# Chebyshev propagations two and three with fp16 pairs in place of bf16 triples

## The reference, cut to what matters

```python
deg = segment_sum(ones, src)                       # out-degree
dis = where(deg > 0, rsqrt(max(deg, 1)), 0)
wn  = -(dis[src] * dis[dst])
prop = lambda h: segment_sum(wn[:, None] * h[src], dst)

T0 = h                                             # relu(layernorm(x))
T1 = prop(T0)                                      # first propagation
T2 = 2 * prop(T1) - T0                             # second
T3 = 2 * prop(T2) - T1                             # third
feats = [sum(T[k] @ w[k]) + b for w, b in ((w2, b2), (w3, b3), (w4, b4))]
# softmax over the three, concatenate, fuse, batch norm, relu, add x
```

## Time and profile before

| | |
|---|---|
| time, median of 3 runs | 1339.63 us (1333.62, 1339.63, 1341.48) |
| span of the profiled execution | 1334.5 us (first to last instruction; no time of its own is listed for it) |
| busy TensorE / VectorE / ScalarE / GpSimd | 1089.8 / 974.4 / 691.7 / 599.0 us |
| propagations k = 1, 2, 3 in the span | from about 1028 to 1242 us |
| line 1324 (the propagations' matmuls, k = 0 to 3) | 2500 matmuls, 19% of the chain of waits |

### The profile page before, as it was taken

How to read it: one execution, slowest core, us unless ns; L and a number is a source line. 1 busy time by engine, 2 the same in 40 slices (tenths; PEclk the granted TensorE clock), 3 DMA queues, 4 the chain that set the end, 5 groups by cost and what they waited for, 6 DMA issues and landing times.

```text
span 1334.5 us, 23321 instructions
## 1 busy us (share of the span) xinstructions
PE 1089.8 (82%) x8345; PEld 633.6 (47%) x8345; DVE 974.4 (73%) x1600; ACT 691.7 (52%) x903; POOL 599.0 (45%) x343
## 2 busy tenths in 40 slices
PE   3878787787796888888788888837996999999893
PEld 2555554454461222222222222214696987788783
DVE  8677888886575999999999999918556535422466
ACT  7555565555446998999898999800000000000221
POOL 8532533422005998999999989960000000000000
PEclk9888878879796999999999999968997999999996
DMA  0100000000144111111112222110011000000201
GB/s 10 30 33 5 7 7 5 8 17 1 40 129 114 36 44 45 47 48 44 45 35 60 53 51 49 45 44 1 1 37 39 25 14 1 22 14 4 66 28 36
DMA packets 98907, 44.80 MB, mean 34 GB/s; under 512 B 85196, under 2 KB 96716, under 8 KB 98672
## 3 DMA queue, kind: packets, MB, share of 16 engines
q1 hardware_dynamic: 97104, 41.58, 11.8%
q0 software_dynamic: 1696, 1.74, 0.5%
HBM read 30.73 MB, written 12.56 MB: 32 GB/s over the span
## 4 chain that ended last, share of the span: by engine, by line
PE 50%; DVE 25%; issue 11%; ACT 5%; POOL 5%; DMA 2%; another core or an unknown queue 2%; SPq 1%; DVEq 0%; ACTq 0%; POOLq 0%
PE PS L1324 19%; DVE Eb L1150 15%; PE PS L553 10%; PE PS L557 8%; POOL Eb L982 3%; DVE Eb L1144 3%; PE PS L1709 3%; PE PS L1332 2%; ACT Eb L1115 2%; PE PS L1074 2%; PE PS L1064 1%; PE PS L1315 1%; ACT Eb L1117 1%; ACT Eb L1119 1%
## 5 line engine op out<-in xcount | busy, mean ns | idle before, releaser
L982 POOL TENSOR_SCALAR Eb<-Eb 128x1024 f32<-128x1024 f32 (+4 forms) x175 | 431.1, 2485 | 74.1 <-ACT Eb L1119 72.8
L1150 DVE SCALAR_TENSOR_TENSOR Eb<-Eb,PS 128x1024 f32<-128x1024 f32 (+4 forms) x350 | 366.7, 1084 | 16.7 <-ACT Eb L1117 10.5
L1324 PE MATMUL PS<-hs,CT 128*128 128x192 f16 (+3 forms) x2500 | 263.3, 267 | 4.0 <-DVE B L1557 1.8
L1119 ACT ACTIVATE Eb<-PS,small 128x1024 f32<-128x1024 f32 (+2 forms) x263 | 251.5, 997 | 28.0 <-PE PS L1064 24.5
L593 ACT ACTIVATE CT<-PS 128x500 f32 x313 | 183.7, 587 | 142.9 <-PE PS L557 135.1
L553 PE MATMUL PS<-mov,oneS 128*128 128x100 f16 x1565 | 184.6, 231 | 76.1 <-issue 71.0
L1324 PEld LDWEIGHTS PS<-hs,CT 128*128 128x128 f16 (+1 forms) x2500 | 227.5, 99 | 37.7 <-DVE SG L1557 2.7
L553 PEld LDWEIGHTS PS<-mov,oneS 128*128 128x128 f16 x1565 | 146.6, 107 | 157.9 <-issue 113.8
L1064 PE MATMUL PS<-Qb,Kb 96*128 96x512 f16 (+3 forms) x700 | 182.8, 364 | 11.1 <-ACT Eb L1119 7.2
L1074 PE MATMUL PS<-Eb,V 128*25 128x512 f32 (+3 forms) x1400 | 169.9, 558 | 3.4 <-DVE Eb L1150 1.8
L435 DVE TENSOR_TENSOR oneS<-iotaX,KL 128x2560 f16<-128x2560 int16 x80 | 120.1, 1501 | 71.6 <-PE PS L557 69.0
(11 more groups left out here) (258 smaller groups left out, 1006.6 us busy)
## 6 DMA issues: line engine op xcount, KB each, us to landing
Kb<-kd SPq DMA_DIRECT2D x168, 96.0 KB, 2.4
qd<-QH SPq DMA_DIRECT2D x12, 192.0 KB, 2.7
kd<-QH SPq DMA_DIRECT2D x12, 192.0 KB, 3.1
hs<-t_d SPq DMA_DIRECT2D x12, 192.0 KB, 2.5
Qb<-qd SPq DMA_DIRECT2D x4, 384.0 KB, 3.9
CT<-x_d SPq DMA_DIRECT2D x1, 1200.0 KB, 7.6
x_d<-B SPq DMA_DIRECT2D x6, 192.0 KB, 1.9
t_d<-A SPq DMA_DIRECT2D x6, 192.0 KB, 1.8
```

The source lines that it names most:

```text
L982: g.tensor_scalar(e, e, ELO, None, ALU.max).then_inc(S("floored"), 1)
L1119: a.activation(e, ps, ACT.Exp, scale=K.unsc[0:r, :]).then_inc(S("score_read"), 1)
L1150: v.scalar_tensor_tensor(out=e, in0=e, scalar=EHI, in1=cn, op0=ALU.min, op1=ALU.mult).then_inc(S("weighed"), 1)
L1324: m = p.matmul(bank(t % FIRST)[0:r, 0:w], K.CT[:, a, 128 * t:128 * t + r], hs[:, a, :, :].rearrange("p k d -> p (k d)"), start=(a == 0), s ...
```

## The change

In k = 2 and 3 the features are now given as two fp16 parts, 192 columns, as in k = 0 and 1. The scale is not the constant 4096 but a power of two for each of the two propagations, from a bound on the size of the values:

- `degrees` also finds the largest `dis` and the largest `dis` times in-degree of each partition (`K.peak`), three operations.
- k = 1's `first_term` finds the smallest value of each group's input (`K.tops`), and one more reduction follows after the seventh group.
- `turn_peaks` on TensorE, after `prop_first`, turns `K.peak` into a row in bank 6 (two transposes for k = 1, one for k = 2).
- `peak_row` on VectorE, after tile 0 of k = 1 and of k = 2, reduces that row to one number and works out the scale and its inverse with single-element operations.
- `spread_scale` on TensorE, after tile 7 (t == 1 of the loop), copies both to all partitions with a matmul; `keep_scale` on VectorE, after tile 3, takes them to SBUF (`K.up`).
- `split` takes the scale from `K.up` for k = 2 and 3: two operations in place of four. `later_term` multiplies by the inverse.

```diff
 def alloc_prop(K, st):
-    K.HS = [sb(st, "hs%d" % i, [128, NT, 3, D], BF16) for i in range(2)]
...
+    K.H0 = sb(st, "hs0", [128, 3 * NT * D // 2], F32)
+    K.HP = [K.H0[:, 0:NT * D].bitcast(F16).rearrange("p (t k d) -> p t k d", k=2, d=D), sb(st, "hs1", [128, NT, 2, D], F16)]
...
     def prop_mm(k, t, groups):
-        hs, w = K.HP[k] if k < 2 else K.HS[k % 2][:, :, :, :], D * parts(k)
+        hs, w = K.HP[k % 2], 2 * D
...
+    def turn_peaks(k):
+        p.wait_ge(S("peaks"), k)
+        for i in range(2 if k == 1 else 1):
+            m = p.transpose(bank(6)[0:1, 128 * i:128 * i + 128], K.peak[:, i:i + 1], K.identf[:, :])
+        m.then_inc(S("peaks_turned"), 1)
+
+    def spread_scale(k):
+        p.wait_ge(S("rise"), k)
+        p.matmul(bank(6)[:, 256:258], K.row1[:, :], K.rise[:, 4:6], start=True, stop=True).then_inc(S("scale_spread"), 1)
+
     for k in range(1, 4):
         for g in range(NG):
             prop_first(k, g)
+        if k < 3:
+            turn_peaks(k)
         for t in range(NT):
             if t + FIRST < NT:
                 prop_rest(k, t + FIRST)
+            if t == 1 and k < 3:
+                spread_scale(k)
...
+    v.memset(K.row1[:, :], 1.0)
...
         v.tensor_tensor(dis, pf[:, 2, :], pf[:, 0, :], ALU.mult).then_inc(step, own.up())
         v.wait_ge(step, own.n)
+        v.tensor_tensor(pf[:, 0, :], dis, K.degd, ALU.mult).then_inc(step, own.up())
+        v.tensor_reduce(K.peak[:, 1:2], dis, AX.X, ALU.max).then_inc(step, own.up())
+        v.wait_ge(step, own.n)
+        v.tensor_reduce(K.peak[:, 0:1], pf[:, 0, :], AX.X, ALU.max).then_inc(S("peaks"), 1)
...
     def split(src, k, g):
         n = tiles(g)
-        o = [K.HS[k % 2][:, 4 * g:4 * g + n, i, :] for i in range(3)]
-        tr = TR[:, 0:n, :]
-        v.tensor_copy(o[0], src).then_inc(step, own.up())
...
-        v.tensor_tensor(tr, src, o[0], ALU.subtract).then_inc(step, own.up())
...
-        v.tensor_copy(o[1], tr).then_inc(step, own.up())
...
-        v.tensor_tensor(o[2], tr, o[1], ALU.subtract).then_inc(S("split_" + FIRST_KEYS[k]), 1)
+        up = UP if k < 2 else K.up[:, k - 2, 0:1]
+        o = [K.HP[k % 2][:, 4 * g:4 * g + n, i, :] for i in range(2)]
+        v.tensor_scalar(o[0], src, up, None, ALU.mult).then_inc(step, own.up())
+        v.wait_ge(step, own.n)
+        v.scalar_tensor_tensor(out=o[1], in0=src, scalar=up, in1=o[0], op0=ALU.mult, op1=ALU.subtract
+                               ).then_inc(S("split_" + FIRST_KEYS[k]), 1)
...
+        v.tensor_reduce(K.tops[:, g:g + 1], SG[:, g % 2, 0:n, :].rearrange("p t d -> p (t d)"), AX.X, ALU.min).then_inc(step, own.up())
         split(SG[:, g % 2, 0:n, :], 2, g)
...
     def later_term(k, out, g):
...
-        v.tensor_tensor(SG[:, s, 0:n, :], SG[:, s, 0:n, :], bcast_in(K.ndis[:, 1, sl], n, D), ALU.mult).then_inc(step, own.up())
+        v.scalar_tensor_tensor(out=SG[:, s, 0:n, :], in0=SG[:, s, 0:n, :], scalar=K.up[:, k - 2, 1:2],
+                               in1=bcast_in(K.ndis[:, 1, sl], n, D), op0=ALU.mult, op1=ALU.mult).then_inc(step, own.up())
...
     for t in range(NT):
         prop_out(B[:, t, :], 1, t)
+        if t == 0:
+            peak_row(1)
+        if t == 3:
+            keep_scale(1)
         if t % 4 == 3 or t == NT - 1:
             first_term(t // 4)
+    v.tensor_reduce(K.peak[:, 0:1], K.tops[:, 0:NG], AX.X, ALU.min).then_inc(S("peaks"), 1)
     for t in range(NT):
         prop_out(sgt(t), 2, t)
+        if t == 0:
+            peak_row(2)
+        if t == 3:
+            keep_scale(2)
```

More of the change, by code:

```diff
@@ L1198, in alloc_prop @@
     K.A = sb(st, "A", [128, NT, D], F32)
-    K.HS = [sb(st, "hs%d" % i, [128, NT, 3, D], BF16) for i in range(2)]
-    K.HP = [h[:, :, :, :].rearrange("p t k d -> p (t k d)").bitcast(F16)[:, 0:NT * 2 * D]
-            .rearrange("p (t k d) -> p t k d", k=2, d=D) for h in K.HS]
+    K.H0 = sb(st, "hs0", [128, 3 * NT * D // 2], F32)
+    K.HP = [K.H0[:, 0:NT * D].bitcast(F16).rearrange("p (t k d) -> p t k d", k=2, d=D), sb(st, "hs1", [128, NT, 2, D], F16)]
+    K.tops = sb(st, "tops", [128, NG + 1], F32)
+    K.peak = sb(st, "peak", [128, 2], F32)
+    K.rise = sb(st, "rise", [1, 8], F32)
+    K.up = sb(st, "up", [128, 2, 2], F32)
+    K.row1 = sb(st, "row1", [1, 128], F32)
     K.TR = sb(st, "TR", [128, 4, D], F32)
@@ L1207, in alloc_prop @@
     K.ndis = K.small[:, 25:75].rearrange("p (k t) -> p k t", k=2)
-    H0 = K.HS[0][:, :, :, :].rearrange("p t k d -> p (t k d)").bitcast(F32)
+    H0 = K.H0
     off = 2 * NT * D // 2
@@ L1240 @@
 UP = 4096.0
+TOP_H = 9.8
 PI = 3.1415927410125732
-def parts(k):
-    return 2 if k < 2 else 3
 def prop_gpsimd(g, K):
@@ L1488, in split @@
         n = tiles(g)
[L1489 to L1496, removed]
-        o = [K.HS[k % 2][:, 4 * g:4 * g + n, i, :] for i in range(3)]
-        tr = TR[:, 0:n, :]
-        v.tensor_copy(o[0], src).then_inc(step, own.up())
-        v.wait_ge(step, own.n)
-        v.tensor_tensor(tr, src, o[0], ALU.subtract).then_inc(step, own.up())
-        v.wait_ge(step, own.n)
-        v.tensor_copy(o[1], tr).then_inc(step, own.up())
-        v.wait_ge(step, own.n)
-        v.tensor_tensor(o[2], tr, o[1], ALU.subtract).then_inc(S("split_" + FIRST_KEYS[k]), 1)
+        up = UP if k < 2 else K.up[:, k - 2, 0:1]
+        o = [K.HP[k % 2][:, 4 * g:4 * g + n, i, :] for i in range(2)]
+        v.tensor_scalar(o[0], src, up, None, ALU.mult).then_inc(step, own.up())
+        v.wait_ge(step, own.n)
+        v.scalar_tensor_tensor(out=o[1], in0=src, scalar=up, in1=o[0], op0=ALU.mult, op1=ALU.subtract
+                               ).then_inc(S("split_" + FIRST_KEYS[k]), 1)
         v.wait_ge(S("split_" + FIRST_KEYS[k]), g + 1)
@@ L1556, in prop_out @@
         v.wait_ge(S("propped"), 25 * k + t + 1)
-        v.tensor_reduce(dst[0:r, :], K.bank(t % FIRST)[0:r, 0:D * parts(k)].rearrange("p (k d) -> p d k", d=D), AX.X, ALU.add
+        v.tensor_reduce(dst[0:r, :], K.bank(t % FIRST)[0:r, 0:2 * D].rearrange("p (k d) -> p d k", d=D), AX.X, ALU.add
                         ).then_inc(S("prop_read"), 1)
@@ L1601, in prop_vector @@
     v.wait_ge(S("x3_out"), 16 * NG)
+    v.wait_ge(S("peaks"), 1)
     v.tensor_scalar(K.ndis[:, 0, :], dis, -1.0 / UP, None, ALU.mult).then_inc(step, own.up())
@@ L1613, in first_term, with peak_row, keep_scale @@
         v.wait_ge(step, own.n)
+        v.tensor_reduce(K.tops[:, g:g + 1], SG[:, g % 2, 0:n, :].rearrange("p t d -> p (t d)"), AX.X, ALU.min).then_inc(step, own.up())
         split(SG[:, g % 2, 0:n, :], 2, g)
+    def peak_row(k):
+        r, bits = K.rise, K.rise[:, :].bitcast(I32)
+        v.wait_ge(S("peaks_turned"), k)
+        if k == 1:
+            v.tensor_reduce(r[:, 0:2], K.bank(6)[0:1, 0:256].rearrange("p (k c) -> p k c", k=2), AX.X, ALU.max
+                            ).then_inc(step, own.up())
+            v.wait_ge(step, own.n)
+            v.scalar_tensor_tensor(out=r[:, 2:3], in0=r[:, 0:1], scalar=TOP_H, in1=r[:, 1:2], op0=ALU.mult, op1=ALU.mult
+                                   ).then_inc(step, own.up())
+            v.wait_ge(step, own.n)
+        else:
+            v.tensor_reduce(r[:, 3:4], K.bank(6)[0:1, 0:128], AX.X, ALU.min).then_inc(step, own.up())
+            v.wait_ge(step, own.n)
+            v.scalar_tensor_tensor(out=r[:, 2:3], in0=r[:, 3:4], scalar=-2.0, in1=r[:, 0:1], op0=ALU.mult, op1=ALU.mult
+                                   ).then_inc(step, own.up())
+            v.wait_ge(step, own.n)
+            v.tensor_scalar(r[:, 2:3], r[:, 2:3], TOP_H, None, ALU.add).then_inc(step, own.up())
+            v.wait_ge(step, own.n)
+        v.tensor_tensor(r[:, 2:3], r[:, 2:3], r[:, 1:2], ALU.mult).then_inc(step, own.up())
+        v.wait_ge(step, own.n)
+        v.tensor_scalar(r[:, 2:3], r[:, 2:3], 1e-12, 1e30, ALU.max, ALU.min).then_inc(step, own.up())
+        v.wait_ge(step, own.n)
+        v.tensor_scalar(bits[:, 3:4], bits[:, 2:3], 23, None, ALU.logical_shift_right).then_inc(step, own.up())
+        v.wait_ge(step, own.n)
+        v.tensor_scalar(bits[:, 6:7], bits[:, 3:4], -1.0, 268.0, ALU.mult, ALU.add).then_inc(step, own.up())
+        v.tensor_scalar(bits[:, 7:8], bits[:, 3:4], 14.0, None, ALU.subtract).then_inc(step, own.up())
+        v.wait_ge(step, own.n)
+        v.tensor_scalar(bits[:, 4:6], bits[:, 6:8], 23, None, ALU.logical_shift_left).then_inc(S("rise"), 1)
+    def keep_scale(k):
+        v.wait_ge(S("scale_spread"), k)
+        v.tensor_copy(K.up[:, k - 1, :], K.bank(6)[:, 256:258]).then_inc(step, own.up())
+        v.wait_ge(step, own.n)
     def later_term(k, out, g):
```

## The result

The changed kernel takes 1292.05 us (median of 4 runs, 1290.41 to 1293.93) where the one before takes 1339.03 (four runs on that chip, 1333.62 to 1341.48). The ratio is 0.965 with a 95% interval of 0.9624 to 0.9676: 47 us less. The forecast was 1290.6 in 1283 to 1299.

The account below looks back on a forecast made before the run. The prediction took TensorE's matmul rate, set by columns, to bound the propagations. Its terms, -50.1 - 0.4 + 0.7 + 0.5 + 0.3 = -49.0 us, took 1339.6 to 1290.6 us, range 1283 to 1299.

Parts of the forecast that it names:

- Matmuls, 50.1 us: In k = 2 and 3, 1250 matmuls go from 123.0 to 82.9 ns each, 50.1 us less.
- Turn from k = 1 to 2, 0.3 less: VectorE's path from the term to the read of tile 24 goes from 3.16 to 2.87 us.
- Turn from k = 2 to 3, nothing: VectorE gains 1.03 us but TensorE finishes tile 24 1.0 us faster, so its wait stays at 1.58 us.
- New instructions of TensorE, 0.7: Three transposes at 0.11 us and two spreads at 0.2 us add 0.7 us in all.
- Wait for peak_row, 0.5: In k = 1 and 2, tile 7 waits for VectorE's delayed read of tile 1; 0.5 us for both.
- Spread behind tile 7: VectorE waits for it after tile 3; tiles 8 and 9 cover TensorE with 0.9 us to spare before tile 10.
- Join of the weights, 0.3: In k = 3, the first join of weight products waits 0.3 us for a load, 1.8 with the slowest load.
- The degrees, 0: Three more small operations, 0.6 us, before VectorE's first read of k = 0 are hidden; at worst 0.3 us.
- the weight load as the bound: Rival: weight loads bound k = 2 and 3, say at 103 ns; gain only 25 us, 1315 us; chance 0.02.
- VectorE's stream: Rival: delays in k = 2 and 3, say VectorE setting the pace, give back all 49 us; 1335 to 1342; chance 0.015.
- The lower clock after a short wait: Rival: new short waits in the propagations lower TensorE's clock, 1.9 us a time; 1294 to 1299 us; chance 0.09.
- rival 2: TensorE's clock drops for a while after new short waits, twice to four times, 4 to 8 us; chance 0.09.

Follow-up runs that it names:

- e1: The kernel before, with matmuls of k = 2 and 3 taking only two of the three bf16 parts (192 columns); ratio 0.9631 to the kernel before.
- e3: The changed kernel with 288 columns again in the matmuls of k = 2 and 3, scale and two-part split kept; ratio 0.9988 to the kernel before.
- e6: The changed kernel with nine more single-number multiplications in peak_row, twice; 1283.04 us in one run.
- e9: The changed kernel with tile 0 last in the first group of k = 1 to 3 and bias loads before weight loads; ratio 0.9615 to the kernel before.
- e10: The changed kernel once more, unedited, on the same chip as e11; 1276.28 us, ratio 0.9627 to the kernel before.
- e11: The kernel of e9 once more, unedited, on the same chip as e10; 1272.67 us, ratio 0.9605 to the kernel before.
- e4: The changed kernel with 128 columns in the matmuls of k = 2 and 3; 1249.13 us in one run.
- e5: The changed kernel with 96 columns in the matmuls of k = 2 and 3, the second part left out; 1239.22 us in one run.

## Why the prediction was right, point by point

- **Matmuls, 50.1 us.** Right: 82.8 ns in the changed kernel, and e1 and e3 show from both sides that the columns carry all but some 2 us of the gain.
- **Turn from k = 1 to 2, 0.3 less.** 0.4 measured: 2.75 us where 2.87 had been summed up. A scalar read from memory costs 0.06 on each of the two parts, as taken from the earlier trace rows (0.41 and 0.62 us for 0.36 and 0.56); the reduction over 384 numbers took the 0.55, and the operation behind it, which does not need its result, began 0.07 before it ended.
- **Turn from k = 2 to 3, nothing.** Right: 1.60 us of wait for 1.61.
- **New instructions of TensorE, 0.7.** Mis-sized: 0.95. The transposes took the 0.33, but the spreads 0.31 each, where 0.2 had been taken without a row.
- **Wait for peak_row, 0.5.** Mis-sized: none. In k = 1 the chain took 1.47 us (1045.71 to 1047.18) in place of 1.85. The operations themselves were shorter, 0.14 us on one number where those of the earlier trace rows on 128x2 took 0.17, so that they came every 0.175 in place of 0.20. Two of them (lines 1652 and 1653) do not depend on each other and came 0.07 apart, and the reads began 0.08 us before the last one had ended; the sum had charged each of these steps in full. That brings the read of tile 1 to its end just before tile 7; e6 shows that 0.2 us is all the slack there was.
- **Spread behind tile 7.** Right: VectorE waited 2.15 us for it, and TensorE never for tile 4.
- **Join of the weights, 0.3.** 0.34 us, and for the load named, as e9 shows.
- **Sum, 49.0.** 48.7 in the stretch. That it is so close is in part luck. The 0.5 for peak_row was too much; the spreads cost 0.25 more than taken, the first 150 matmuls of k = 1 were 0.14 longer, and in k = 3, where no transposes stand ahead of tile 6, TensorE stood 0.1 us for the read of tile 0, which no term had. The medians are 47.0 apart, the spans 45.9; the 2.4 us by which the stretch began later are of the size by which this beginning varies between profiles (e10 and e11).
- **The degrees, 0.** TensorE ran its 100 matmuls there in the 8.42 us of the earlier trace rows, so what was added was hidden; it was 0.4 us and not 0.6 (from the start of these matmuls to the first read 1.45 us for 1.05).

Of the rivals, the weight load as the bound is refuted down to 42.6 ns (e4, e5), and VectorE's stream ends a whole propagation later than TensorE would only at 96 columns, by its late start (e5). The lower clock after a short wait did not happen in the changed kernel (1.41 and 1.60 us), but did in e1 and e4 (2.41 and 2.27 us): its waits were 0.7 us short of the shortest wait with a lower clock behind it, and the price of 1.6 us a time is what rival 2 had put at 1.9. What the prediction names from the Trainium skill, TensorE: Matmul & The Clock Gate, section HAM oscillation, is told there of matmul bursts that are shorter than the waits between them. Between two turns here TensorE works for some 50 us, so the rows at the turns are another case and do not contradict that section, though the prediction says that they do.

## What to carry to other kernels

A stream of these matmuls without gaps in the chain of waits cost what its columns cost, from 96 to 288 of them, and its rate for fewer columns could be read from another place in the same kernel. What shortens TensorE's last tile before a turn does not shorten the in-order work that the turn waits for: read the last bank first, or give TensorE something first that does not need it. A chain of small operations put between two reads is free only as far as one tile's matmuls reach. From the rows of such operations elsewhere that could be worked out to 0.4 us; to do better, look which of them wait for each other.

## What the runs showed that was not expected

- A pair of a 128-column fp16 weight load and a 96-column matmul was sustained at 42.6 ns over 175 in a row (e5).
- In the propagations k = 1 to 3, waits of 1.36 to 1.82 us before matmuls of line 1325 (1324 before) had a granted clock of 1.00 behind them in all profiles here; waits of 2.27 and 2.41 us had 0.83 and 0.88 over the next 10 and 14 us, which cost 1.6 us each (e4, e1). Behind the wait of 4.43 us in e5 it was 0.69 over 9 us.
- The kernel before is 12 to 13 us slower on the chip of the result than on the others, and a wait of this size shows at the start of the propagation stage's first layer. On the first chip VectorE stood 21.32 and 21.42 us before line 1539 (before and changed), in e10 and e1 8.26 and 6.62 us. In e10 the product that this line reads ended 0.04 us earlier. In the changed kernel's first profile VectorE had read the gathered values of this group at 882.51 and TensorE's product ended at 895.52, yet the line began at 904.09. The profile names no engine of this core for the end of that wait (`remote`), so what makes the one chip slower stays open.

Here is that row for the changed kernel on the first chip, then for e10; in brackets the idle time and what ended it:

```profile
904.09 0.56 DVE L1539 SCALAR_TENSOR_TENSOR TR<-PS,small 128x384 f32<-128x384 f32 x1 [21.42 <-remote]
```

```profile
888.97 0.56 DVE L1539 SCALAR_TENSOR_TENSOR TR<-PS,small 128x384 f32<-128x384 f32 x1 [8.26 <-PE PS L1316]
```
